# Convolution stage: the query, norm and outer products in the first column group of TensorE, issued between the taps; keys and values in two banks of PSUM

## The reference

```python
branches = [bn_relu(conv(x, w, pad, dil))         # 4 x 32 channels: 1x1, and 3x3 with dilation 6, 12, 18
            for ...]
x_q = concatenate(branches, axis=1)               # 128 channels
Q = wq x_q + bq                                   # 16 rows over N = 16384 pixels
K = wk x + bk                                     # 16 rows
V = wv x + bv                                     # 128 rows
Qn, Kn = Q / |Q|, K / |K|                         # norms over the 16 rows, pixel by pixel
tailor = 1 / (N + Qn . (Kn.sum(-1) + EPS))
mat = einsum('bmn,bcn->bmc', Kn, V)               # 16 x 128 for each image
out = gamma * (V.sum(-1) + Qn . mat) * tailor
```

## Time and profile before

| | us |
|---|---|
| median of 3 runs | 18219.49 (18219.25 to 18220.81) |
| profiled execution, its own time | 18229.67 |
| its span, first to last instruction | 18227.6 |
| TensorE busy in the span | 15233.1 (84%) |
| VectorE busy | 14628.5 (80%) |
| GpSimd busy | 13648.5 (75%) |
| ScalarE busy | 10286.6 (56%) |

### The profile page before, as it was taken

The page is one execution under the profiler, slowest core; times in us unless marked ns, Lnnn a source line. Parts: engine busy times, 40 slices in busy tenths (PEclk is TensorE's granted clock), DMA queues, the critical chain, the costliest instruction groups (busy, mean ns, idle before and its releaser), DMA issues. The chain is left out here.

```text
span 18227.6 us, 188137 instructions
## 1 busy us (share of the span) xinstructions
PE 15233.1 (84%) x40250; PEld 5585.0 (31%) x40250; DVE 14628.5 (80%) x14056; ACT 10286.6 (56%) x14202; POOL 13648.5 (75%) x5902
## 2 busy tenths in 40 slices
PE   8999999777788888888888888888888888888876
PEld 2333333222233333333333333333333333233322
DVE  1111111599999999999999999999999999999952
ACT  1222222466666666666666666666666666666642
POOL 0000000399999999999999999999999999999940
PEclk9999999899998888888888888888888888888865
DMA  1101110244444444444444444444444444444445
GB/s 38 33 27 32 29 28 21 85 161 162 159 155 164 162 157 161 163 159 162 156 162 157 164 160 158 163 158 159 159 164 159 157 164 162 155 157 164 162 180 210
DMA packets 508191, 2499.22 MB, mean 137 GB/s; under 512 B 53097, under 2 KB 164938, under 8 KB 226651
## 3 DMA queue, kind: packets, MB, share of 16 engines
q1 hardware_dynamic: 489723, 2419.71, 35.8%
q10 hardware_dynamic: 18208, 76.11, 1.1%
HBM read 2325.05 MB, written 170.57 MB: 137 GB/s over the span
## 5 line engine op out<-in xcount | busy, mean ns | idle before, releaser
L718 POOL TENSOR_TENSOR hc<-h,c_all 128x1024 f32<-128x1024 f32 x4096 | 9526.9, 2355 | 278.5 <-PE y_ps L959 271.3
L959 PE MATMUL y_ps<-hc,ident 128*128 128x512 f32 x16392 | 8002.9, 632 | 932.1 <-POOL hc L718 931.8
L834 ACT ACTIVATE d_a<-dt,a_neg 128x512 f32<-128x512 f32 x8194 | 5596.3, 688 | 4252.4 <-DVE h L1063 4203.0
L1063 DVE TENSOR_TENSOR_SCAN h<-d_a,h,dbx_v 128x512 f32<-128x512 f32 x4960 | 6100.8, 1268 | 24.4
L959 PEld LDWEIGHTS y_ps<-hc,ident 128*128 128x128 f32 x16392 | 3158.7, 202 | 5895.4 <-issue 3803.8
L707 POOL TENSOR_TENSOR dbx_p<-dtx,b_all 128x1024 f32<-128x1024 f32 x1536 | 3616.0, 2354 | 185.1 <-DVE h L1063 184.5
L1063 DVE TENSOR_TENSOR_SCAN h<-d_a,h,dbx_p 128x512 f32<-128x512 f32 x2976 | 3660.7, 1267 | 43.1 <-ACT d_a L834 38.5
L1050 DVE TENSOR_TENSOR dbx_v<-dtx_ps,b_all 128x1024 f32<-128x1024 f32 x2560 | 3021.6, 1207 | 13.1 <-issue 9.5
L463 POOL MEMSET ident_f<- 128x128 f32 x1 | 0.2, 205 | 3350.9 <-POOLq L44 3350.9
L346 DVE RECIPROCAL k_inv<-k_nrm 128x4 f32<-128x4 f32 x256 | 45.5, 178 | 2686.2 <-ACT k_nrm L211 2686.2
L271 PE MATMUL conv_ps<-image,w_taps 128*32 128x512 f32 x11520 | 1775.2, 594 | 0.0
(11 more groups left out here) (128 smaller groups left out, 10841.0 us busy)
## 6 DMA issues: line engine op xcount, KB each, us to landing
b_all<-bc_dram SPq DMA_DIRECT2D x1028, 1024.0 KB, 6.9
c_all<-bc_dram SPq DMA_DIRECT2D x1025, 1024.0 KB, 4.7
o_dram<-o_sb SPq DMA_DIRECT2D x257, 256.0 KB, 7.4
o_t<-o_dram SPq DMA_DIRECT2D x64, 1024.0 KB, 9.9
out<-r_t ACTq DMA_DIRECT2D x64, 1024.0 KB, 9.2
image<-in_x SPq DMA_DIRECT2D x91, 512.0 KB, 4.1
un<-un_dram SPq DMA_DIRECT2D x516, 34.0 KB
bc_dram<-low_bc SPq DMA_DIRECT2D x257, 64.0 KB, 4.5
```

Source lines behind the costliest of these rows:

```text
L718: nc.gpsimd.tensor_tensor(hc[:, n % HC], h[:, n], c_all[:, n // CG % 2, n % CG].unsqueeze(1).broadcast_to([128, 2, CH]), ALU.mult).then_in ...
L834: nc.scalar.activation(d_a[:, half], dt[:, p, half], ACT.Exp, scale=a_neg[:, half, n:n + 1]).then_inc(a_done, 1)
L959: last = nc.tensor.matmul(y_ps[:, half], ident[:], hc[:, n % HC, half], start=False, stop=(n == S - 1))
L1063: nc.vector.tensor_tensor_scan(h[:, n, half], d_a[:, half], dbx, zero_col[:] if first else h[:, n, half, CH - 1:CH], ALU.mult, ALU.add).th ...
```

## The change

The query, norm and outer products of chunk r-1 are issued between the taps of chunk r: the query behind tap 0, the four outer products behind taps 3, 5, 7 and 9, the norm behind the tap that has three more after it (tap 20 of 0 to 23). All three now write PSUM partitions of group 0: the norm's matrix of ones has 32 columns in place of 64 and 128 rows in place of 16 (the squared query's rows 16 to 127 are cleared once), and its result has a bank of its own, `s_ps`. Keys and values use two banks in place of four, so `kv` waits for VectorE to have read those of the chunk before (`v_done`, k + 2); `mat_ps` has two banks. Its wait for `mat_done` is as before. In the last round of an image the order is query, outer products, norm. The norm also waits for `s_done`.

```diff
--- before.py
+++ after.py
@@ -64,12 +64,12 @@
         bn_mi = sb("bn_mi", [C, 1])
         bn_shift = sb("bn_shift", [C, 1])
         bn_eps = sb("bn_eps", [C, 1])
-        ones_m = sb("ones_m", [M, 64])
+        ones_m = sb("ones_m", [128, 32])
         zero_chunk = sb("zero_chunk", [KU, CH])
         x_q = sb("x_q", [C, CH])
         q_sb = sb("q_sb", [M, 2, CH])
-        s_sb = sb("s_sb", [65, 2, CH])
-        q_sq = sb("q_sq", [M, CH])
+        s_sb = sb("s_sb", [1, 2, CH])
+        q_sq = sb("q_sq", [128, CH])
         k_sb = sb("k_sb", [128, SUB, M])
         k_sq = sb("k_sq", [128, SUB, M])
         k_n2 = sb("k_n2", [128, SUB])
@@ -85,9 +85,10 @@
         den_inv = sb("den_inv", [128, 128])
 
         conv_ps = ps("conv_ps", [128, 2, CH])
-        kv_ps = ps("kv_ps", [128, 2, 2, CH])
+        kv_ps = ps("kv_ps", [128, 2, CH])
+        mat_ps = ps("mat_ps", [KU, 2, CH])
         qs_ps = ps("qs_ps", [128, CH])
-        mat_ps = ps("mat_ps", [128, CH])
+        s_ps = ps("s_ps", [128, CH])
 
         weights = sem("weights")
         cleared = sem("cleared")
@@ -130,7 +131,7 @@
                              (b_q[:], t["b_q"]), (bn[:], t["bn"])):
                 sp.dma_start(dst, src).then_inc(weights, 16)
 
-            sp.wait_ge(cleared, 5)
+            sp.wait_ge(cleared, 6)
             for i in range(4):
                 rows = slice(i * 32, i * 32 + 32)
                 sp.dma_start(image[:, PAD + 32 * i:PAD + 32 * i + 32, PAD:PAD + W],
@@ -183,6 +184,7 @@
             pool.memset(image[:], 0.0).then_inc(cleared, 1)
             pool.memset(zero_chunk[:], 0.0).then_inc(cleared, 1)
             pool.memset(ones_m[:], 1.0).then_inc(cleared, 1)
+            pool.memset(q_sq[:], 0.0).then_inc(cleared, 1)
             pool.memset(kn1[:], 1.0).then_inc(cleared, 1)
             pool.memset(v1[:], 1.0).then_inc(cleared, 1)
             for p in range(2):
@@ -197,6 +199,7 @@
             act.sem_inc(bn_done, 2)
             act.sem_inc(s_done, 1)
             act.wait_ge(set_up, 5)
+            act.wait_ge(cleared, 6)
 
             def relu(b, r, p):
                 act.wait_ge(conv_done, b * NCH + r + 1)
@@ -218,14 +221,14 @@
                 act.wait_ge(u_stored[p], 32 * (b * (NCH // 2) + j + 1))
                 nc.scalar.activation(q_sb[:, p], qs_ps[0:M, :], ACT.Identity, bias=b_q[:]).then_inc(q_done, 1)
                 act.wait_ge(s2_mm, k + 1)
-                nc.scalar.activation(q_sq[:], qs_ps[0:M, :], ACT.Square, bias=b_q[:]).then_inc(sq_done, 1)
+                nc.scalar.activation(q_sq[0:M], qs_ps[0:M, :], ACT.Square, bias=b_q[:]).then_inc(sq_done, 1)
                 act.wait_ge(s2_mm, k + 2)
-                nc.scalar.activation(s_sb[64:65, p], qs_ps[64:65, :], ACT.Sqrt).then_inc(s_done, 1)
+                nc.scalar.activation(s_sb[:, p], s_ps[0:1, :], ACT.Sqrt).then_inc(s_done, 1)
                 act.wait_ge(q_done, k + 1)
                 act.wait_ge(s_done, k + 2)
                 c0 = (b * NCH + r) * CH
                 act.dma_start(uq[0:M, bass.ds(c0, CH)], q_sb[:, p]).then_inc(u_stored[p], 16)
-                act.dma_start(uq[M:KU, bass.ds(c0, CH)], s_sb[64:65, p]).then_inc(u_stored[p], 16)
+                act.dma_start(uq[M:KU, bass.ds(c0, CH)], s_sb[:, p]).then_inc(u_stored[p], 16)
 
             with act.Fori(0, B) as b:
                 with act.Fori(0, NCH // 2) as j:
@@ -245,53 +248,52 @@
         @block.tensor
         def _(pe):
             pe.wait_ge(weights, 16 * 7)
-            pe.wait_ge(cleared, 5)
+            pe.wait_ge(cleared, 6)
             pe.sem_inc(q_mm, 1)
             pe.sem_inc(s2_mm, 1)
 
             def kv(b, r, p):
                 k = b * NCH + r
-                pe.wait_ge(v_done, k + 1)
+                pe.wait_ge(v_done, k + 2)
                 for j in range(SUB):
-                    last = nc.tensor.matmul(kv_ps[:, p, j // 2, (j % 2) * (M + C):(j % 2 + 1) * (M + C)],
+                    last = nc.tensor.matmul(kv_ps[:, j // 2, (j % 2) * (M + C):(j % 2 + 1) * (M + C)],
                                             image[:, PAD + ROWS * r + j, PAD:PAD + W], w_kv[:], start=True, stop=True)
                 last.then_inc(kv_done, 1)
 
-            def conv(b, r, p):
+            def center(b, r, p):
                 k = b * NCH + r
                 pe.wait_ge(bn_done, k + 1)
                 y0 = r * ROWS + PAD
                 nc.tensor.matmul(conv_ps[:, p], w_center[:], image[:, y0:y0 + ROWS, PAD:PAD + W],
                                  start=True, stop=False, skip_group_check=True)
 
-                steps = [(n, i) for n, (dy, _) in enumerate(TAPS) for i, d in enumerate(DIL)
-                         if -ROWS < r * ROWS + dy * d < H]
-                for n, i in steps:
-                    y1, x1 = y0 + TAPS[n][0] * DIL[i], PAD + TAPS[n][1] * DIL[i]
-                    last = nc.tensor.matmul(conv_ps[BR * (i + 1):BR * (i + 2), p], w_taps[:, i, n, :],
-                                            image[:, y1:y1 + ROWS, x1:x1 + W],
-                                            start=False, stop=(n == 7), skip_group_check=True)
-                last.then_inc(conv_done, 1)
-
-            def query(b, r, p):
+            def tap(r, p, n, i):
+                y1, x1 = r * ROWS + PAD + TAPS[n][0] * DIL[i], PAD + TAPS[n][1] * DIL[i]
+                return nc.tensor.matmul(conv_ps[BR * (i + 1):BR * (i + 2), p], w_taps[:, i, n, :],
+                                        image[:, y1:y1 + ROWS, x1:x1 + W],
+                                        start=False, stop=(n == 7), skip_group_check=True)
+
+            def query(b, r):
                 k = b * NCH + r
                 pe.wait_ge(bn_done, k + 3)
                 pe.wait_ge(s_done, k + 1)
                 nc.tensor.matmul(qs_ps[0:M, :], w_q[:], x_q[:], start=True, stop=True).then_inc(q_mm, 1)
 
-            def query_norm(b, r, p):
+            def query_norm(b, r):
                 k = b * NCH + r
                 pe.wait_ge(sq_done, k + 1)
-                nc.tensor.matmul(qs_ps[64:128, :], ones_m[:], q_sq[:], start=True, stop=True).then_inc(s2_mm, 1)
-
-            def outer(b, r, p):
+                pe.wait_ge(s_done, k + 1)
+                nc.tensor.matmul(s_ps[0:32, :], ones_m[:], q_sq[:], start=True, stop=True).then_inc(s2_mm, 1)
+
+            def outer(b, r, p, j):
                 k = b * NCH + r
-                pe.wait_ge(kn_done, k + 2)
-                pe.wait_ge(mat_done, k + 1)
-                for j in range(SUB):
-                    last = nc.tensor.matmul(mat_ps[0:KU, 0:C + 1], kn1[:, p, j, :], v1[:, p, j, :],
-                                            start=(j == 0), stop=(j == SUB - 1))
-                last.then_inc(mat_mm, 1)
+                if j == 0:
+                    pe.wait_ge(kn_done, k + 2)
+                    pe.wait_ge(mat_done, k + 1)
+                last = nc.tensor.matmul(mat_ps[:, p, 0:C + 1], kn1[:, p, j, :], v1[:, p, j, :],
+                                        start=(j == 0), stop=(j == SUB - 1))
+                if j == SUB - 1:
+                    last.then_inc(mat_mm, 1)
 
             with pe.Fori(0, B) as b:
                 loaded(pe, b)
@@ -301,13 +303,27 @@
 
                     if r < NCH:
                         kv(b, r, p)
-                    if r > 0:
-                        query(b, r - 1, 1 - p)
+                        center(b, r, p)
+                        steps = [(n, i) for n, (dy, _) in enumerate(TAPS) for i, d in enumerate(DIL)
+                                 if -ROWS < r * ROWS + dy * d < H]
+                    else:
+                        steps = []
+                    for at, (n, i) in enumerate(steps):
+                        last = tap(r, p, n, i)
+                        if r > 0:
+                            if at == 0:
+                                query(b, r - 1)
+                            if at in (3, 5, 7, 9):
+                                outer(b, r - 1, 1 - p, (at - 3) // 2)
+                            if at == len(steps) - 4:
+                                query_norm(b, r - 1)
                     if r < NCH:
-                        conv(b, r, p)
-                    if r > 0:
-                        query_norm(b, r - 1, 1 - p)
-                        outer(b, r - 1, 1 - p)
+                        last.then_inc(conv_done, 1)
+                    else:
+                        query(b, r - 1)
+                        for j in range(SUB):
+                            outer(b, r - 1, 1 - p, j)
+                        query_norm(b, r - 1)
 
         @block.vector
         def _(dve):
@@ -320,7 +336,7 @@
             nc.vector.tensor_tensor(bn_mi[:], bn[:, 2:3], bn_inv[:], ALU.mult).then_inc(set_up, 1)
             dve.wait_ge(set_up, 4)
             nc.vector.tensor_tensor(bn_shift[:], bn[:, 1:2], bn_mi[:], ALU.subtract).then_inc(set_up, 1)
-            dve.wait_ge(cleared, 5)
+            dve.wait_ge(cleared, 6)
             dve.sem_inc(v_done, 2)
             dve.sem_inc(kinv_done, 1)
```

(14 more changed lines are left out.)

## The result

The changed kernel takes 17307.42 us (median of 4 runs, 17304.74 to 17317.48) against 18219.92 us of the kernel before (4 runs): ratio 0.950, interval 0.9484 to 0.9517. The prediction was 17305. Its profiled execution took 17308.57 us, span 17306.8.

A forecast was written before the change was run, and what follows sets the result against it. TensorE, running a chunk's products one after another, bounds the first stage; kv, center and taps remain, 9.10 us a chunk. Saving 912 + 11 - 10 + 2 = 915 us gives 17305, range 17270 to 17345, reaching up to 17500 through ScalarE's chain.

The forecast's parts named there:

- The main sum: First stage, chunks 1 to 31 of eight images: period falls from 12.86 to 9.10 us, saving 912 us.
- The overlap with the taps: Query, norm and four outer products, 2.6 us in column group 0 beside the taps, were taken to cost 0.
- Rival 2: Column group 0 isn't free: its products hold up the taps, period 10.4 us, total some 17630; chance 0.14.
- Rival 3: Each product in group 0 drains the taps around it: period 14.6 us, slower, some 18670; chance 0.04.
- Rival 4: Products land behind the taps in effect and only the wait goes: 0.2% or less; chance 0.02.
- Rival 1: ScalarE's chain from norm to query becomes the bound: period 9.8 us, total some 17480; chance 0.13.
- The gain at the image changes: Between images, the earlier norm lets the next kv start sooner: 1.5 us at each of seven changes, 11 us.
- kv at about S + 8.6: At an image change, the next image's keys and values start 8.6 us after S, where it was 10.16.
- one chain of 4.09 us: After an image's last chunk, the next image's kv starts 4.09 us after norm 31, which waits for q_sq.
- 10 us for the clock: After image changes the granted clock may come back later: 1.5 us lost on each of seven, 10 in all.
- The end of the stage: At the end of the first stage, 2 us are gained.
- 11 - 10 + 2 = +3: Small terms beside the 912 us: image changes gain 11 us, clock loses 10, end of stage gains 2.

## Why the prediction was right

The main sum came out term by term. The stage is 912.0 us shorter, and chunks 1 to 31 give 912.4 of it (the small rest, as told below, comes to about 0): chunk 1 went from 12.18 to 9.04 (forecast 9.10), the 29 next from 12.85 to 9.09 (from 12.86 to 9.10), chunk 31 from 8.41 to 6.48 (6.52). The overlap with the taps was priced at 0, and the run with four more products shows 0. Which part of the gain needs interleaving, the prediction did not see: being of the taps' shape in an idle group gives 235 us by itself, and being written between the taps the remaining 677. Taken in the other order, the wide norm between the taps has a stage 631 us shorter than before (3375.7 to 2744.5), and the taps' shape adds the last 281. Each part is worth more when it comes second.

The rivals fell as follows. Rival 2 (group 0 isn't free) fell by the four products more. Rival 3 (drains) is real for another shape, 1.1 us a chunk for one product of 64 columns, and absent for 16, 17 and 32 columns over 128 rows. Whether the 64 columns or the 16 rows do it wasn't told apart. (Its period in the prediction should be 9.10 - 7.02 + 12.4 = 14.5, not 14.6; the verdict on it is the same.) Rival 4 (the products land behind the taps in effect) fell by the total and by the timeline. Rival 1 (ScalarE's chain) stands right behind the forecast: norm behind tap 23 in place of 20 costs 0.72 us a chunk, 180 us in all.

**Where a step was wrong and it didn't show.** The prediction has: "The norm is placed behind tap 20 of 24; tap 20's first pass starts ... 1.84 before S", followed by 3.93 or 3.69 us to the query. The norm started 2.66 before S, the start of kv (1011.89, kv at 1014.55), 0.8 too early for the forecast, and from its start to the root it was 1.94 us (to 1013.83), in place of the 1.10 that the 3.93 taken over from the kernel before holds; in the chunk of the earlier trace rows its timeline has the root at

```profile
...
1016.12 0.59 ACT L223 ACTIVATE s_sb<-qs_ps 1x512 f32<-1x512 f32 x1 [7.83 <-PE qs_ps L285]
```

behind a norm at 1015.02. The two errors cancel, and that is luck: the root starts 0.72 before S where the forecast's terms give 0.74, and the query 2.05 or 2.11 behind S where it had 2.08 or 2.09.

The prediction has the norm start with tap 20, behind which it is written. The trace has it a round of taps before that: the first passes of taps 15, 16 and 17 start at 1011.84, 1011.86 and 1011.88, the norm at 1011.89, those of the next round at 1012.70, 1012.72 and 1012.74. It is so in all 192 chunks with 24 taps: 33 passes of taps have started when the norm does. With the norm behind tap 14 it is 21 in all 192 (it starts at 1008.39, and tap 14 0.85 later, at 1009.24), and at the old place, behind all 24 taps, 39.

The same is in chunk 1 of the earlier trace rows. An image's first chunks have few taps of the wide dilations, and here four taps of group 1, not three, are written ahead of the first of group 2. The passes of group 1 start at 480.54, 480.99, 481.42, 481.85 and 482.28, each 0.59 to 0.62 long; so the 0.43 us that the prediction gives a pass is from start to start. Groups 2 and 3 start at 482.29 and 482.30, 0.01 behind the first pass of the third tap, ahead of its second pass (482.71) and of the fourth tap (483.14). From there on three passes start in each 0.43: 482.71, 482.75 and 482.75, then 483.14, 483.18 and 483.18. That is three abreast.

And the root is late because the norm's semaphore comes only when the products written ahead of it are done: tap 20's second pass starts at about 1013.16 and ends at 1013.75, and the trace's record of semaphores has the norm's at 1013.81, 0.88 behind its own modelled end; the root starts at 1013.83. With the norm moved to tap 14 the root moved to that tap's end, and with tap 23 to that one's. Three positions show it.

**Terms mis-sized.** The gain at the image changes was put at 1.5 us each: taps' end to kv stayed 10.3 us (10.34 before, 10.31 after, means of seven). The step "kv at about S + 8.6" failed. What the prediction read as one chain of 4.09 us behind the norm holds the jump back, and in the changed kernel the jump ends 1.3 to 1.5 us behind the end of an instruction packet that starts 2.9 to 3.3 us into it, near the end of the load. The load ended 7.7 us behind S before (467.27) and 7.6 after (352.43), so starting the jump 2 us earlier gave nothing.

Against this gain stood 10 us for the clock, 1.5 at each change. Measured was half of that. Chunk 0 went from 8.14 to 8.63 us in the mean, 3.9 us over eight images: the first image's, which follows no change, became 1.0 shorter (why is not shown), and the seven others 0.70 longer each, 4.9 us. After an image change the granted clock stays on the lower level into chunk 0, for 3.1 us behind kv in the mean before (1.5 to 4.6) and for 4.6 in the changed kernel (3.0 to 6.1), by the trace's clock records. At the first change it is 6.1 us, to 361.2:

```profile
...
355.00:359.00 4.00, 3.87 (x10) 2.42 (x10) 1.17 (x4) 0.00 (x0) 0.00 (x0) 0.50 0.66 179
359.00:364.00 5.00, 5.00 (x28) 1.27 (x30) 0.00 (x0) 0.00 (x0) 0.00 (x0) 0.78 0.32 85
```

The 14 changes of image of the two kernels lie on one line: chunk 0 takes 6.48 us and 0.48 for each microsecond on the lower level, to 0.03 us. So a microsecond at half the clock costs half a microsecond here.

The end of the stage gave 3.8 us where 2 were put. With 0.5 us lost ahead of the first kv these terms come to about 0, where 11 - 10 + 2 = +3 was forecast. That this small sum is close is luck too: its two large terms were both too large, with opposite signs.

For a pass of the outer products the prediction has 0.107 us, a figure that no run shows. In the kernel before they start 0.11 us apart (six steps from 1016.14 to 1016.81), and 0.11 beside the taps too (1008.40, 1008.51, 1008.62 and 1008.73).

## What to carry to other kernels

Before moving a product, look at its shape: one of the taps' own shape (16, 17 or 32 columns over all 128 rows here) in an idle column group cost nothing beside three others (1.3 us of the stage for 660 us of work), and started ahead of products written before it (0.85 us ahead of the tap it was written behind); one of 64 columns over 16 rows stopped all groups (1.1 us a chunk). The semaphore of such a product came by its written place, not by its start (0.9 us behind the product's own modelled end): put a product whose consumer is on the critical chain ahead of as many others as its inputs allow. When one stage of a long program is at issue, compare the stage's own length in the profiles: here 25 us were plain in the stage and lost in the spread of the totals. And look for what differs from execution to execution even there, here 3.4 us by the clock.

## What was not expected of the hardware

- A product of a free column group started 1.26 us ahead of taps written before it (1.86 us before kv, with all 24 taps written ahead of it), and its semaphore came only when those were done, 0.9 us behind its own modelled end.
- TensorE's jump back at the end of an image takes 3.3 to 3.9 us with the DMA engines quiet or the load nearly done, and 5.5 to 5.8 us in the changed kernel, where 1.5 MB are being loaded: its 16 KB instruction packet starts 0.9 to 1.3 us into the jump in the one case, and 2.9 to 3.3 in the other.
- A first chunk of 6.48 us grows by 0.48 us for each microsecond that the clock is still on the lower level.
- The untouched stages took between 14835 and 14862 us in the twelve profiled executions, 26 us apart, with the same instructions.
